# Attention of a six-stage network: the value matmuls of a whole step in a row, and the squares of the scores shared by three engines

## The reference

```python
scores = jnp.einsum('bhqd,bhkd->bhqk', q, k) * hs ** (-0.5)
p = jax.nn.softplus(scores)
p = p * p
p = p * jnp.tril(jnp.ones((t, t), dtype=p.dtype))
attn = p / (jnp.sum(p, axis=-1, keepdims=True) + 1e-09)
out = jnp.einsum('bhqk,bhkd->bhqd', attn, v)
```

## Time and profile before

| | |
|---|---|
| median of 3 runs | 1729.88 us (1729.46 to 1731.93) |
| the profiled execution | 1730.23 us, span of its instructions 1728.2 us |
| busy share of the span | TensorE 96%, VectorE 69%, ScalarE 49%, GpSimd 35% |
| TensorE's granted clock, mean | 0.99 |
| attention in the span | about 275 to 754 us |
| squares on VectorE (line 1420) | 176, 262.9 us busy |
| squares on GpSimd (line 1483) | 112, 221.4 us busy |
| softplus on ScalarE (line 1404) | 288, 280.7 us busy |

### The profile page before, as it was taken

How to read it: one execution, slowest core, us unless ns; L and a number is a source line. 1 busy time by engine, 2 the same in 40 slices (tenths; PEclk the granted TensorE clock), 3 DMA queues, 4 the chain that set the end, 5 groups by cost and what they waited for, 6 DMA issues and landing times. The chain is left out here.

```text
span 1728.2 us, 28920 instructions
## 1 busy us (share of the span) xinstructions
PE 1650.6 (96%) x11188; PEld 1149.8 (67%) x11188; DVE 1192.8 (69%) x2418; ACT 849.5 (49%) x1324; POOL 601.8 (35%) x478
## 2 busy tenths in 40 slices
PE   8999888999999999989999999998999999899999
PEld 7888774333333333368888777786777777677787
DVE  5455897666566656656556888876877777778876
ACT  4332686555555555643332232227888887522220
POOL 0002116555555555550004422211465555411111
PEclk9999999999999999999999999998999999999999
DMA  5000266636355463300001100002232323200000
GB/s 169 2 1 13 74 195 136 85 50 94 55 82 67 70 78 57 42 2 13 1 0 37 32 1 1 1 1 64 93 105 99 99 99 100 98 13 13 25 25 25
DMA packets 57016, 95.79 MB, mean 55 GB/s; under 512 B 7760, under 2 KB 29488, under 8 KB 56880
## 3 DMA queue, kind: packets, MB, share of 16 engines
q1 hardware_dynamic: 55920, 93.35, 24.5%
q10 hardware_dynamic: 960, 0.59, 0.1%
HBM read 76.88 MB, written 17.04 MB: 54 GB/s over the span
## 5 line engine op out<-in xcount | busy, mean ns | idle before, releaser
L1404 ACT ACTIVATE att_weights<-ps 128x1024 f32<-128x1024 f32 (+1 forms) x288 | 280.7, 976 | 193.2 <-PE ps L1345 106.0
L1420 DVE TENSOR_TENSOR att_weights<-att_weights 128x1024 f32<-128x1024 f32 (+1 forms) x176 | 262.9, 1504 | 86.8 <-ACT att_weights L1404 86.8
L1366 PE MATMUL ps<-att_weights,att_v_ones 64*32 64x64 f32 (+5 forms) x2048 | 286.8, 398 | 13.9 <-DVE v L1441 13.9
L927 DVE SCALAR_TENSOR_TENSOR X<-ps,moe_gsel,X 128x256 f32<-128x256 f32 x512 | 246.1, 483 | 72.3 <-PE ps L48 50.1
L1483 POOL TENSOR_TENSOR att_weights<-att_weights 128x1024 f32<-128x1024 f32 x112 | 221.4, 1979 | 202.7 <-ACT att_weights L1404 202.0
L48 PE MATMUL ps<-w_experts_hi,moe_xh 128*128 128x512 f32 x512 | 204.1, 399 | 0.0
L48 PE MATMUL ps<-w_experts_hi,moe_xl 128*128 128x512 f32 x512 | 203.2, 397 | 0.0
L48 PE MATMUL ps<-w_experts_lo,moe_xh 128*128 128x512 f32 x512 | 201.5, 393 | 0.0
L1366 PEld LDWEIGHTS ps<-att_weights,att_v_ones 128*32 128x32 f32 (+1 forms) x2048 | 81.8, 108 | 132.4 <-issue 83.6
L424 ACT ACTIVATE ffn_gates<-ps,ffn_gate_bias 128x512 f32<-128x512 f32 x72 | 49.5, 688 | 148.2 <-PE ps L48 126.6
L48 PEld LDWEIGHTS ps<-w_experts_hi,moe_xh 128*128 128x128 f32 x512 | 96.1, 188 | 24.3
(11 more groups left out here) (281 smaller groups left out, 3742.3 us busy)
## 6 DMA issues: line engine op xcount, KB each, us to landing
ssm_lb<-decays SPq DMA_DIRECT2D x32, 512.0 KB, 4.7
ssm_rise<-decays SPq DMA_DIRECT2D x28, 512.0 KB, 3.9
qk_parts<-qkv_part SPq DMA_DIRECT2D x32, 384.0 KB, 2.8
q_stack<-qk_parts SPq DMA_DIRECT2D x64, 128.0 KB, 4.7
k_stack<-qk_parts SPq DMA_DIRECT2D x64, 128.0 KB, 8.7
att_q_stack<-qk_parts SPq DMA_DIRECT2D x64, 128.0 KB, 4.8
att_k_stack<-qk_parts SPq DMA_DIRECT2D x64, 128.0 KB, 8.3
out<-X SPq DMA_DIRECT2D x7, 512.0 KB, 3.0
```

Of the source, the lines that this page charges most:

```text
L927: dve.scalar_tensor_tensor(out=x, in0=ring[:, e // 2, (e % 2) * C:(e % 2 + 1) * C], scalar=gsel[:, s, j, e:e + 1], in1=x, op0=ALU.mult, op ...
L1366: ins = pe.matmul(O(qb)[h * 2 * HD:(h + 1) * 2 * HD, q0:q0 + w], values, Wt[rows, u % WU, t, c:c + w], start=kj == 0 and part == FULL, sto ...
L1404: act.activation(Wt[:, u % WU, 0:n], scores(u)[:, 0:n], ACT.Softplus).then_inc(plus_done, 1)
L1420: dve.tensor_tensor(wt, wt, wt, ALU.mult).then_inc(sq_dve, 1)
```

## The change

Three things change, all in attention.

`value_unit` becomes `value_step`. It waits for the squares of all units of the step and then issues the step's products without a break, so that the four heads' products stand next to each other. In the body TensorE now issues the scores of both units of a step (still 7 ahead), then the values of the step, then the turns that fall on its units. The numbers of matmuls stay as they were.

The table `engine_of` takes the place of `on_pool`: in every pass the units 1, 3, 6, 8, 10, 13 and 15 go to GpSimd, the half-width units 4 and 17 to ScalarE, the other nine to VectorE. Three semaphores count the squares, one for each engine.

ScalarE squares its two units with an activation function, in place, after the softplus of the next unit.

```diff
@@ -1284,9 +1284,9 @@

-    on_pool = lambda u: u % 5 in (1, 3)
-    pool_squares = [sum(on_pool(x) for x in range(u)) for u in range(NU + 1)]
-    dve_squares = [u - pool_squares[u] for u in range(NU + 1)]
+    BY_DVE, BY_POOL, BY_ACT = range(3)
+    engine_of = [BY_ACT if BANKS[u % PU] == 1 else BY_POOL if u % PU in (1, 3, 6, 8, 10, 13, 15) else BY_DVE for u in range(NU)]
+    squares = [[sum(engine_of[x] == e for x in range(u)) for u in range(NU + 1)] for e in range(3)]

@@ -1318,7 +1318,7 @@
         s_done, plus_done, pv_done = sem("s_done"), sem("plus_done"), sem("pv_done")
-        sq_pool, sq_dve = sem("sq_pool"), sem("sq_dve")
+        sq_dve, sq_pool, sq_act = squared = sem("sq_dve"), sem("sq_pool"), sem("sq_act")
         oT_done, o_turned, den_done, rec_done, o_done = (sem(n) for n in ("oT_done", "o_turned", "den_done", "rec_done", "o_done"))
@@ -1345,28 +1345,24 @@

-            def value_unit(i, u):
-                m = step_of[u]
+            def value_step(i, m):
                 s, (qb, last, products) = m // PS, pass_steps[m % PS]
-                if u % PU == 0:
+                base = s * PU
+                if m % PS == 0:
                     pe.wait_ge(v_copied, 2 * (2 * i + s + 1))
-                if products[0][1:3] == (0, u % PU) and products[0][-1] != UPPER:
+                if products[0][1] == 0 and products[0][-1] != UPPER:
                     pe.wait_ge(o_done, (i * 2 + s) * BLOCKS + qb + 1)
                     if qb == 0:
                         pe.matmul(O(qb), ident16[:, :], neg[:, 0:1].broadcast_to([P, BANK]), start=True, stop=False)
-                if on_pool(u):
-                    pe.wait_ge(sq_pool, i * pool_squares[NU] + pool_squares[u + 1])
-                else:
-                    pe.wait_ge(sq_dve, i * dve_squares[NU] + dve_squares[u + 1])
+                for u in range(base + products[0][2], base + last + 1):
+                    pe.wait_ge(squared[engine_of[u]], i * squares[engine_of[u]][NU] + squares[engine_of[u]][u + 1])
                 for h, kj, unit, t, c, q, w, part in products:
-                    if unit == u % PU:
-                        q0 = q - qb * BANK
-                        rows = slice(h % 2 * HALF, (h % 2 + 1) * HALF) if part == UPPER else slice(0, P)
-                        values = va_up[rows, s, kj, h // 2] if part == UPPER and h % 2 else va[rows, s, kj, h]
-                        ins = pe.matmul(O(qb)[h * 2 * HD:(h + 1) * 2 * HD, q0:q0 + w], values,
-                                        Wt[rows, u % WU, t, c:c + w], start=kj == 0 and part == FULL, stop=part == UPPER and kj == (qb + 1) * GT - 1)
-                if last == u % PU:
-                    ins.then_inc(pv_done, 1)
+                    q0 = q - qb * BANK
+                    rows = slice(h % 2 * HALF, (h % 2 + 1) * HALF) if part == UPPER else slice(0, P)
+                    values = va_up[rows, s, kj, h // 2] if part == UPPER and h % 2 else va[rows, s, kj, h]
+                    ins = pe.matmul(O(qb)[h * 2 * HD:(h + 1) * 2 * HD, q0:q0 + w], values,
+                                    Wt[rows, (base + unit) % WU, t, c:c + w], start=kj == 0 and part == FULL, stop=part == UPPER and kj == (qb + 1) * GT - 1)
+                ins.then_inc(pv_done, 1)

@@ -1376,11 +1372,14 @@
             def body(i, first=False, last=False):
-                for u in range(NU):
-                    if not (last and u + AHEAD >= NU):
-                        score_unit(i, u + AHEAD)
-                    value_unit(i, u)
-                    outputs_at(u, BLOCK_UNITS, NU, TURN_LAG, i, first, turn_output)
+                for m in range(NS):
+                    begin, end = step_end[m - 1] + 1 if m else 0, step_end[m] + 1
+                    for u in range(begin, end):
+                        if not (last and u + AHEAD >= NU):
+                            score_unit(i, u + AHEAD)
+                    value_step(i, m)
+                    for u in range(begin, end):
+                        outputs_at(u, BLOCK_UNITS, NU, TURN_LAG, i, first, turn_output)
                 if last:
@@ -1407,9 +1406,19 @@
             act.sem_inc(plus_done, SU)
+
+            def square(i, u):
+                act.wait_ge(plus_done, SU + i * NU + u + 1)
+                wt = Wt[:, u % WU, 0:BANKS[u % PU]]
+                act.activation(wt, wt, ACT.Square).then_inc(sq_act, 1)
+
             for i in range(BODIES):
                 for u in range(NU):
                     softplus(i, u)
+                    if u and engine_of[u - 1] == BY_ACT:
+                        square(i, u - 1)
+                if engine_of[NU - 1] == BY_ACT:
+                    square(i, NU - 1)

@@ -1443,7 +1452,7 @@
                 for u in range(NU):
-                    if not on_pool(u):
+                    if engine_of[u] == BY_DVE:
                         square(i, u)
@@ -1477,7 +1486,7 @@
                 for u in range(NU):
-                    if on_pool(u):
+                    if engine_of[u] == BY_POOL:
                         pool.wait_ge(plus_done, SU + i * NU + u + 1)
```

## The result

The changed kernel takes 1626.16 us (median of 4 runs, 1625.58 to 1627.60) against 1730.91 for the kernel before (median of 4); the ratio is 0.9396 with a 95% interval of 0.938 to 0.9413. The forecast was 1633, the range 1612 to 1690. The profiled execution took 1625.58 us.

The account below looks back on a forecast made before the run. TensorE bounds attention at 30.05 us a pass; afterwards the squares' floor of 23.0 plus 0.6 for bubbles gives 23.6. Sixteen passes save 103 us, less about 6 at the ends: 1730 - 97 = 1633 us, range 1612 to 1690.

Parts of the forecast that it names:

- Four heads together: TensorE value matmuls: four heads' streams overlap fully, a step takes 0.99 us, saving 7.9 us a pass.
- the estimate of 1.2 us a step: TensorE value work if the skill page's 2.38 times carried on to four tiles; 1.7 us more TensorE time a pass.
- Rivals one, three and four: TensorE's four value streams overlap in part (1655, chance 0.13), only in twos (1710, 0.09), or not at all (1934, 0.05).
- The squares late next: VectorE's and GpSimd's squares run one after the other, 1.09 and 1.75 us each, making a floor of 23.0 us a pass.
- The half-width squares: Two squares a pass move to ScalarE, taken as 0.60 us each, without a second table load.
- nobody waits: ScalarE's half-width squares delay no one, since their reader stands seven score units back.
- without that part of the change the floor would be 1.1 us a pass higher: Worth of moving the two half-width squares to ScalarE: 1.1 us a pass off the squares' floor.
- The sum: Whole-kernel forecast: passes fall from 30.05 to 23.6 us, 103 us, less about 6: 97 us saved, 1633.
- for such bubbles I add 0.6 us: Idle time per pass from TensorE's wait for the division that frees an output bank, raising 23.0 to 23.6 us.
- head and tail: About 6 us of the saving lost at attention's ends: late first squares, and a last body bound by squares.
- Loads and ScalarE: Query and key stack loads stay hidden (16.9 us against a pass of 23); ScalarE needs about 19.6 us a pass.
- Rival two: Output chain in VectorE's in-order queue decides: about 1.25 us lost per output block, pass 25.5 us, 1663; chance 0.12.

Follow-up runs that it names:

- e8: Changed kernel with the output bank cleared four times instead of once a pass, 0.64 us more TensorE work a pass; 1626.68 us.
- e9: Changed kernel, same squares table, with copy, sums and division of an output block earlier in VectorE's queue (lags 5, 8, 8 for 7, 9, 10); 1625.86 us.
- e3: Changed kernel with one wide square of each pass moved from GpSimd to VectorE (6 and 10 for 7 and 9); 1628.18 us.
- e1: Changed kernel with the old table of squares, half-width ones on VectorE, so only the grouping of value matmuls is new; 1660.16 us.
- e6: Changed kernel with 5 GpSimd and 11 VectorE squares a pass, and sums and division earlier (lags 7, 8, 8); 1632.11 us.
- e7: Changed kernel with 5 GpSimd and 11 VectorE squares a pass, and copy, sums and division earlier (lags 5, 8, 8); 1612.16 us.
- e4: Changed kernel with two wide squares of each pass moved from GpSimd to VectorE (5 and 11 for 7 and 9); 1624.99 us.
- e12: Changed kernel with the old table of squares (half-width ones on VectorE) and early copy, sums and division (lags 5, 8, 8); 1657.91 us.
- e11: Changed kernel with 3 GpSimd and 13 VectorE squares a pass, and early copy, sums and division (lags 5, 8, 8); 1620.72 us.
- e5: Changed kernel, same squares table, with sums and division of an output block earlier in VectorE's queue (lags 7, 8, 8); 1629.21 us.
- e10: Changed kernel with 4 GpSimd and 12 VectorE squares a pass, and early copy, sums and division (lags 5, 8, 8); 1630.41 us.

## Why the prediction was right

**Four heads together.** Right in mechanism and size: 1.00 us a step for the 0.99 taken from the half-width rows, nothing near 1.89. Four streams of 128 rows overlap fully, though no row had shown it: the half-width rows, of which each stream is 64 high, were a good guide. TensorE's busy time in the pass from 392.30 to 415.15 us is 20.96 us for the forecast 21.2. The Trainium skill ("TensorE: Matmul & The Clock Gate", Measured speedup vs the span model) has 2.38 times for three column tiles; the estimate of 1.2 us a step that I worked out from it is not borne out here, since four tiles take 1.00 us, as long as two. Rivals one, three and four fall with it.

**The squares late next.** Right: with 2.84 us for a pair of squares, 1.75 + 1.09 as read from two collisions before, the changed pass is the sum of its squares within 0.2 us (22.85 or 23.01 in most passes, for 23.0). Their means rose by waiting for each other, as said. e8 and e9 show it from the other sides: more TensorE work costs nothing, an earlier output chain gains nothing. e3, with a shorter sum, shows it in part: its passes without a fall of the clock take 22.65 us on the mean, for its floor of 22.3.

**The half-width squares.** The two on ScalarE take 624 ns each for the 0.60 taken, with 0.3 us of idle time before all of them, and no table load stands in attention's trace. TensorE's weight loads wait 3.0 us for them from 285 to 630 us, where "nobody waits" was forecast; it does not show in the pass. Their worth was underestimated: the step "without that part of the change the floor would be 1.1 us a pass higher" gave 18 us, e1 shows 34. The floor is not the whole of it: e1's pass of 25.07 lies between its two sums, 24.1 and 26.2, and less of VectorE's other work falls beside GpSimd's squares (21.9 of 40.8 us from 285 to 630, for 31.7 of 44.4). Falls of the clock may add to it. How much of this is the half-width squares, the order of the wide ones and the clock stays open.

**The sum.** 6.8 us too slow. The term that failed is "for such bubbles I add 0.6 us": the pass is 23.04, on the floor of 23.0, so 16 x (23.6 - 23.04) = 9 us were added for nothing. TensorE's waits for the division are there (13.3 us from 285 to 630), but the squares run on meanwhile. 16 x (30.05 - 23.04) = 112 us, less 104.5 measured, leaves 7.7 where I had 6 for head and tail; as the projection starts 106.4 us earlier, 5.8 of it are head and tail and 1.9 lie in the rest of the program.

**Loads and ScalarE** stayed off the path, as forecast: ScalarE is busy 285.03 of 374 us, and no wait names a transfer.

**Rival two**, the output chain, did not decide the changed kernel but was close: in e6, where the squares need 21.7 us, it holds the pass, as e7 shows by moving the copy; in e4 the falls of the clock have a share.

## What to carry to other kernels

When the bound of a stage is relieved, work out the sum of every resource behind it, shared ones too: two engines that exclude each other count as one, with the times read from collisions and not from means. If the next bounds lie within a few per cent of each other, moving one alone gains nothing; e4 and e9 gained nothing singly and e7, which is both, 14 us. Before a kernel that gains nothing is read as a second bound, its granted clock by pass belongs beside it: by the estimate above, e3 hid half of its gain there. An engine whose queue holds both shared and unshared work reaches the sum of the shared part only if the unshared part falls into the other's turns.

## What was not expected of the hardware

TensorE's clock fell to its lower level twice within the changed kernel's passes, though it is busy 91% of attention; before, its mean over attention is 1.00. The windows view, the stretch before such a fall and the stretch after it:

```profile
554.30:566.00 11.70, 9.48 (x141) 4.28 (x140) 11.66 (x10) 9.94 (x11) 11.70 (x5) 1.00 0.95 116
566.20:569.60 3.40, 3.40 (x21) 1.16 (x14) 3.40 (x3) 0.51 (x1) 3.34 (x3) 0.50 0.00 0
```

and TensorE's timeline there:

```profile
566.04 1.83 PE L1363 MATMUL ps<-att_weights,att_v_ones 128*32 128x512 f32 x8 [2.26 <-DVE v L1450]
```

TensorE had waited 2.26 us for the division; then the granted clock is 0.50, the level of 1.2 GHz, and a step's values take 1.83 us for 1.06. A wait of the same length at 520.02 us has no fall behind it.

What a fall costs depends on what holds the pass. In the changed kernel the pass with this fall takes 24.64 us and the next one 21.56, together 46.20 for the 46.01 of the two before them. In e9 such a pair takes 24.52 + 21.28 = 45.80, twice its steady 22.90. So where the squares hold the pass, the next pass makes up for the fall; e8, with a clock of 1.00 over all 15 passes, has a mean pass of 22.86 us for 23.09 and the same time. Where they don't, as in e3 (lines above), much of the 1.6 us stays. Falls stand in 8 of the 15 passes of e1 and of e12, 5 of e3, 4 of e4 and e6, 3 of e9 and e11, 2 of the changed kernel and e5, 1 of e7 and none of e8 and e10. No run changes the clock alone, so what they cost e1 and e12 is not shown.
